# Column sums in layer 0, a scan in the recurrence: a change to a four-layer graph and feed-forward kernel

## The reference

```python
# layer 0, graph part (x is normalised first, the result is added to x)
h = layer_norm(x, ln_gamma, ln_beta)
agg = einsum('bij,bjh->bih', adj, h)
return x + relu(agg @ W_rel + b_rel + h @ W_root)

# layer 0, feed-forward part: a recurrence over T = 128 steps, batch 64
i_t = sigmoid(xi_t + h @ V_i)
g_t = tanh(xg_t + h @ V_c)
o_t = sigmoid(xo_t + h @ V_o)
c_new = h * c + i_t * g_t
h_new = o_t * tanh(c_new)

# layer 1, graph part: needs a sum over each row of adj
adj_norm = adj / (sum(adj, axis=-1, keepdims=True) + EPS)
```

## Time and profile before

| what | value |
|---|---|
| median of 3 runs | 1869.44 us (1867.50 to 1871.53) |
| span of the profiled execution | 1867.1 us |
| TensorE busy, share of the span | 1627.8 us, 87% |
| VectorE busy, share of the span | 1095.9 us, 59% |
| ScalarE busy, share of the span | 998.9 us, 53% |
| GpSimd busy, share of the span | 786.7 us, 42% |
| mean granted TensorE clock | 0.941 |

### The profile page before, as it was taken

One profiled execution on the slowest core, in us unless ns is written; L12 is line 12 of the kernel. 1 busy time (PEld: TensorE's weight loads), 2 busy tenths in 40 slices (PEclk: granted clock), 3 DMA queues, 4 the chain that ended last, 5 costly groups with the idle time before them and its releaser, 6 DMA issues. The chain is left out here.

```text
span 1867.1 us, 43356 instructions
## 1 busy us (share of the span) xinstructions
PE 1627.8 (87%) x13366; PEld 1314.2 (70%) x13366; DVE 1095.9 (59%) x4199; ACT 998.9 (53%) x3116; POOL 786.7 (42%) x1358
## 2 busy tenths in 40 slices
PE   7978899988859987999998888879999888884995
PEld 5756677767759985788887566679999845553542
DVE  7933433348737777699998755523333377763552
ACT  5854444446636656666665433246666534441663
POOL 6710000014426666111111677745565434554675
PEclk9989999999969999899999799989999989995998
DMA  3200000010014420000000511122222253105331
GB/s 114 84 1 1 1 1 1 1 27 1 1 36 134 123 80 1 2 3 2 2 3 3 156 47 48 62 62 70 72 71 72 56 150 86 58 24 88 100 86 35
DMA packets 125926, 91.76 MB, mean 49 GB/s; under 512 B 23591, under 2 KB 116554, under 8 KB 125701
## 3 DMA queue, kind: packets, MB, share of 16 engines
q1 hardware_dynamic: 109110, 61.89, 12.6%
q0 software_dynamic: 13568, 25.90, 4.3%
q10 hardware_dynamic: 3024, 1.21, 0.4%
HBM read 57.71 MB, written 33.30 MB: 49 GB/s over the span
## 5 line engine op out<-in xcount | busy, mean ns | idle before, releaser
L1361 ACT ACTIVATE FEAT<-BANKS,FEAT 128x128 f32<-128x128 f32 x544 | 155.5, 368 | 82.1 <-PE BANKS L1314 82.1
L1206 POOL DMA_INDIRECT scratch_made<-FEAT x136 | 144.9, 1065 | 122.6 <-DVE FEAT L1500 119.8
L1061 ACT ACTIVATE EXP<-BANKS,NEGMAX 128x128 f32<-128x128 f32 x512 | 139.4, 383 | 59.5 <-DVE NEGMAX L1073 59.5
L440 ACT ACTIVATE gates<-BANKS,EXP 128x64 f32<-128x64 f32 x384 | 97.4, 314 | 112.6 <-PE BANKS L417 112.6
L1314 PE MATMUL BANKS<-FEAT 128*128 128x128 f32 x1088 | 145.5, 277 | 0.0
L1323 PE MATMUL BANKS<-AUX,FEAT 128*128 x1088 | 144.5, 276 | 0.4 <-ACT FEAT L1361 0.4
L417 PEld LDWEIGHTS BANKS<-AUX,EXP 128*128 128x128 f32 x768 | 95.4, 191 | 69.7 <-DVE AUX L464 69.6
L1198 POOL DMA_INDIRECT scratch_sent<-FEAT,POS x128 | 125.1, 977 | 38.3 <-issue 37.5
L990 POOL COPY EXP<-AUX 128x32 f32<-128x32 f32 x256 | 42.5, 211 | 217.8 <-PE BANKS L1036 217.8
L1314 PEld LDWEIGHTS BANKS<-FEAT 128*128 128x128 f32 x1088 | 133.9, 194 | 0.0
L1323 PEld LDWEIGHTS BANKS<-AUX,FEAT 128*128 128x128 f32 x1088 | 133.2, 193 | 0.6 <-issue 0.6
(11 more groups left out here) (367 smaller groups left out, 4196.0 us busy)
## 6 DMA issues: line engine op xcount, KB each, us to landing
EXP<-in_L_ffn_W SPq DMA_DIRECT2D x128, 128.0 KB, 2.1
FEAT<-scratch_sent SPq DMA_DIRECT2D x136, 64.5 KB
EXP<-scratch_made SPq DMA_DIRECT2D x32, 256.0 KB, 3.4
FEAT<-scratch_sent SPq DMA_DIRECT2D x96, 65.5 KB, 1.9
X<-in_x SPq DMA_DIRECT2D x16, 256.0 KB, 2.9
STAGE<-in_adj SPq DMA_DIRECT2D x16, 256.0 KB, 3.3
scratch_sent<-NONE SPq DMA_DIRECT2D x48, 65.5 KB, 3.3
scratch_sent<-FEAT,POS POOLq DMA_INDIRECT x192, 2.3
```

The costliest lines, as they stand in the source:

```text
L440: act.activation(gates[:, at, sp_, :], PS[2 * at + par][:, u * B:(u + 1) * B], f, bias=wr["b" + gate]).then_inc(done, 1)
L1061: last = act.activation(tile(EXS[:, par], 4 * k + n), tile(PS[j], c), ACT.Exp, bias=NEGMAX[:, par, 4 * k + n:4 * k + n + 1])
L1206: pool.indirect_dma_start(out=made2, out_offset=bass.IndirectOffsetOnAxis(ap=XI_I[:, t % R_IN, H:ROW2], axis=0), in_=YO[:, t % R_OUT, :], ...
L1361: last = act.activation(tile(HR[:, t % R_H], c), tile(PS[2 + t % 2], c), ACT.Gelu, bias=BT[:, c, t:t + 1])
```

## The change

The column sums leave the recurrence: TensorE makes them in layer 0, four behind each group's adjacency products, into the same bank 6. In their place the recurrence issues a filler, so that every step has two fillers beside an input product or three without one. On VectorE, `ig` and `cell` become one `tensor_tensor_scan`, which runs along its 128 columns with state = `by` * state + `plus`. Column 2b of `by` is zero and of `plus` is g, so the state becomes g; column 2b + 1 of `by` is i and of `plus` is h times the old cell, so the state becomes the new cell. ScalarE therefore writes i and g, and VectorE `hc`, at every second column of a buffer, and the cell is read at every second column of `made`. GpSimd clears `made` and `by` at the start. The waits written ahead of the scan are `hc`, `it`, `gt`, in this order.

```diff
--- before.py
+++ after.py
@@ -217,6 +217,7 @@
                        "raw2 mv2 var2 rstd2 n2 m2 xn2 x_ps xT")
         adj_v = a["adj"].rearrange("(g b) i j -> g i b j", b=G)
         x_v = a["x"].rearrange("(g b) t h -> g t b h", b=G)
+        ROWSUM = PS[6][:, 0:B]
         PWB = sb("PWB", [P, 2, 2, 2, G])
         NMR = sb("NMR", [P, 2, G])
         NEG = sb("NEG", [P, 2, G])
@@ -368,6 +369,8 @@
                         last = pe.matmul(tile(PS[3], k), tile(WC2[:, par], k), cols(AT, i, GW, k * T, T),
                                          start=False, stop=True, skip_group_check=True)
                     last.then_inc(s.conv, 1)
+                    for k in range(G):
+                        pe.matmul(ROWSUM[:, G * i + k:G * i + k + 1], cols(AT, i, GW, k * T, T), ones[:, 0:1], start=True, stop=True)
 
                 def back(i, par, half):
                     pe.wait_ge(s.relu, i + 1)
@@ -382,20 +385,20 @@
                 unrolled(NG, [(2, hT), (3, back), (2, project), (0, adjacency), (4, xT), (2, conv)])
 
         layer()
-        s = sems("rnn", "zero x_even x_odd g i o gt it ot hc ig c ct h")
+        s = sems("rnn", "zero x_even x_odd g i o gt it ot hc c ct h")
         HS = AUX
-        cell = lb("cell", [P, 2, B])
-        hc = lb("hc", [P, 2, B])
-        ig = lb("ig", [P, 2, B])
-        gates = lb("gates", [P, 3, 2, B])
+        by = lb("by", [P, 2, B, 2])
+        plus = lb("plus", [P, 2, B, 2])
+        made = lb("made", [P, 2, B, 2])
+        gate_o = lb("gate_o", [P, 2, B])
         tanhc = lb("tanhc", [P, 2, B])
         NT = T // STEPS
-        ROWSUM = PS[6][:, 0:B]
         with nc.Block() as block:
             @block.gpsimd
             def _(pool):
                 pool.memset(HS[:, 0:B], 0.0).then_inc(s.zero, 1)
-                pool.memset(cell[:, 1, :], 0.0).then_inc(s.zero, 1)
+                pool.memset(made[:, 1], 0.0).then_inc(s.zero, 1)
+                pool.memset(by[:], 0.0).then_inc(s.zero, 1)
 
             @block.tensor
             def _(pe):
@@ -412,16 +415,14 @@
 
                     for u in range(STEPS):
                         step = j * STEPS + u
-                        pe.wait_ge(s.h if step else s.zero, step if step else 2)
+                        pe.wait_ge(s.h if step else s.zero, step if step else 3)
                         for gate_at, (gate, sem) in enumerate(zip("ico", (s.i, s.g, s.o))):
                             pe.matmul(PS[2 * gate_at + par][:, u * B:(u + 1) * B], wr["V" + gate],
                                       cols(HS, j, STEPS * B, u * B, B), start=False, stop=True,
                                       skip_group_check=True).then_inc(sem, 1)
                         if prefetch and u < 6:
                             inputs(j + 1, 1 - par, u // 2, u % 2)
-                        if step < B:
-                            pe.matmul(ROWSUM[:, step:step + 1], AT[:, step * T:(step + 1) * T], ones[:, 0:1], start=True, stop=True)
-                        for _ in range((2 if prefetch and u < 6 else 3) - (step < B)):
+                        for _ in range(2 if prefetch and u < 6 else 3):
                             pe.matmul(PS[7][:, 0:half], ident[:], cols(FEAT, j, STEPS * B, 0, half), start=True, stop=True)
                 for gate_at in range(3):
                     for part in range(2):
@@ -434,13 +435,15 @@
                 def turn(j, par):
                     for u in range(STEPS):
                         step, sp_ = j * STEPS + u, u % 2
-                        for at, (gate, made, done, f) in enumerate((("i", s.i, s.it, ACT.Sigmoid), ("c", s.g, s.gt, ACT.Tanh),
-                                                                    ("o", s.o, s.ot, ACT.Sigmoid))):
-                            act.wait_ge(made, step + 1)
-                            act.activation(gates[:, at, sp_, :], PS[2 * at + par][:, u * B:(u + 1) * B], f,
+                        for at, (gate, ready, done, f, into) in enumerate((
+                                ("i", s.i, s.it, ACT.Sigmoid, by[:, sp_, :, 1]), ("c", s.g, s.gt, ACT.Tanh, plus[:, sp_, :, 0]),
+                                ("o", s.o, s.ot, ACT.Sigmoid, gate_o[:, sp_, :]))):
+                            act.wait_ge(ready, step + 1)
+                            act.activation(into, PS[2 * at + par][:, u * B:(u + 1) * B], f,
                                            bias=wr["b" + gate]).then_inc(done, 1)
                         act.wait_ge(s.c, step + 1)
-                        act.activation(tanhc[:, sp_, :], cell[:, sp_, :], ACT.Tanh).then_inc(s.ct, 1)
+                        act.activation(tanhc[:, sp_, :], made[:, sp_, :, 1], ACT.Tanh).then_inc(s.ct, 1)
+                act.wait_ge(s.zero, 3)
                 for j in range(NT):
                     turn(j, j % 2)
 
@@ -451,19 +454,18 @@
                         step, q = j * STEPS + u, u % 2
                         if step:
                             v.wait_ge(s.h, step)
-                        v.tensor_tensor(hc[:, q, :], cols(HS, j, STEPS * B, u * B, B), cell[:, 1 - q, :],
+                        v.tensor_tensor(plus[:, q, :, 1], cols(HS, j, STEPS * B, u * B, B), made[:, 1 - q, :, 1],
                                         ALU.mult).then_inc(s.hc, 1)
+                        v.wait_ge(s.hc, step + 1)
+                        v.wait_ge(s.it, step + 1)
                         v.wait_ge(s.gt, step + 1)
-                        v.wait_ge(s.it, step + 1)
-                        v.tensor_tensor(ig[:, q, :], gates[:, 0, q, :], gates[:, 1, q, :], ALU.mult).then_inc(s.ig, 1)
-                        v.wait_ge(s.hc, step + 1)
-                        v.wait_ge(s.ig, step + 1)
-                        v.tensor_tensor(cell[:, q, :], hc[:, q, :], ig[:, q, :], ALU.add).then_inc(s.c, 1)
+                        v.tensor_tensor_scan(made[:, q].rearrange("p b k -> p (b k)"), by[:, q].rearrange("p b k -> p (b k)"),
+                                             plus[:, q].rearrange("p b k -> p (b k)"), 0.0, ALU.mult, ALU.add).then_inc(s.c, 1)
                         v.wait_ge(s.ot, step + 1)
                         v.wait_ge(s.ct, step + 1)
-                        v.tensor_tensor(cols(HS, j, STEPS * B, (u + 1) * B, B), gates[:, 2, q, :], tanhc[:, q, :],
+                        v.tensor_tensor(cols(HS, j, STEPS * B, (u + 1) * B, B), gate_o[:, q, :], tanhc[:, q, :],
                                         ALU.mult).then_inc(s.h, 1)
-                v.wait_ge(s.zero, 2)
+                v.wait_ge(s.zero, 3)
                 for j in range(NT):
                     turn(j, j % 2)
```

## The result

The changed kernel takes 1878.08 us (median of 4 runs, 1874.56 to 1880.98) where the kernel before takes 1870.01 us (median of 4): a ratio of 1.0043 with a 95% interval of 1.0026 to 1.006, so it is slower. The medians differ by 8.1 us, where the prediction forecast 3.7. The execution profiled has a span of 1872.7 us against 1867.1, 5.6 us more. Where these 5.6 us lie is read from the starts of two instructions, the relu of layer 0 and the last multiply of a step of the recurrence, in both kernels (for the last multiply before, see the earlier trace rows).

What follows compares the result with a forecast made beforehand. Layer 0 was taken as bound by a closed loop across several engines, the recurrence by a chain of dependent steps. Terms: 11.0 - 7.3 = +3.7 us, giving 1873.1 us; range 1862 to 1884.

Steps and rivals of the forecast that it cites:

- the worked-out case: Whole kernel: the summed terms give +3.7 us, 1873.1 us, own range 1870 to 1876; chance 0.58.
- (a): Recurrence, before the scan: the late wait costs nothing extra, -5 us in all, 1864; chance 0.08.
- (b): Layer 0: the column sums are absorbed, -7 us in all, 1862; chance 0.05.
- (d): Recurrence activations: ScalarE pays for strided access, +3 to +22 us on top, about 1883; chance 0.13.
- Column sums in layer 0, +11.0 us: Layer 0: sums delay hT and so L313 by 0.73 us; round 6.12 instead of 5.39, 15 x 0.73.
- Fillers, nothing: Recurrence, steps 0 to 63: one more filler each costs nothing unless a step falls below about 2.07 us.
- The scan, 0.425 us: VectorE in the recurrence: scan estimated at two slots a column, 0.425 us, between bounds 0.29 and 0.95.
- (c): Recurrence: the scan runs at the tensor_tensor row, 0.29 us; -13 us in all, 1856; chance 0.08.
- (e): Recurrence: the scan is longer than estimated, 1.3 us per 0.01 us, 1895 at 0.6 us; chance 0.08.
- The wait, 0.10 us: Recurrence, g's end to scan: late semaphore written last, so 0.10 us, not 0.03; saving 0.057 a step, -7.3 us.
- Strides, 0: Recurrence: writing or reading every second word taken as 0, bounds 0 and +22 us.
- lengthened activations: Recurrence, ScalarE: activations stay 0.314 and 0.256 us; the prediction is wrong if they lengthen.

Runs made afterwards that it cites:

- sums_behind_hT: Changed kernel with each group's column sums one round later, behind the next group's hT transposes; 1865.64 us against 1868.06 for the kernel before, ratio 0.999.
- gt_first: Changed kernel with the scan's waits written gt, hc, it; 1862.75 us against 1866.26 for the kernel before, ratio 0.9984.
- it_last: Kernel before, without a scan, with the waits of ig written it, gt instead of gt, it; 1876.72 us against 1866.26, ratio 1.0062.
- ct_first_before: Kernel before with the last multiply's waits written ct, ot instead of ot, ct; 1858.93 us against 1868.14, ratio 0.9943.
- two_waits: Changed kernel with the scan waiting for hc and gt only; 1872.06 us against 1866.24 for the kernel before, ratio 1.0038.
- sums_back: Changed kernel with the column sums in the recurrence again; two executions 1867.50 and 1868.47 us, four 1935 to 1939, beside 1866.26 for the kernel before.
- sums_back_table_early: Changed kernel, column sums back in the recurrence, ScalarE's cleared-buffers wait moved behind its first-gate wait; 1863.24 us against 1868.06 for the kernel before, ratio 0.9977.
- fewer_fillers: Changed kernel with one filler less in each of steps 0 to 63; 1878.52 us against 1868.06 for the kernel before, ratio 1.0054.

## Why the prediction was right, and where it was off

Direction and range hold: slower was the likeliest of the three, at 0.46, and 1878.1 lies within 1862 to 1884. The size does not. The forecast of +3.7 us is under half of the +8.1 measured, and 1878.1 lies outside the 1870 to 1876 to which the worked-out case gave 0.58; the wide range holds because it was drawn to take in rivals (a), (b) and most of (d), and none of them came. The mechanisms of both parts were right. What failed is the size of one term and one term that was missing.

- *Column sums in layer 0, +11.0 us*: measured +10.6, in the change and alone. The place (L313 waits for `hT`) and the round (6.12 forecast, 6.10 measured) hold. Rival (b) falls here; with the sums behind `hT` (sums_behind_hT) it comes true.
- *Fillers, nothing*: right in the step. The room was larger than worked out: at a step of 2.08 us TensorE's loads still wait 0.25 us for h.
- *The scan, 0.425 us*: measured 0.425. The half throughput that the Trainium skill states (DVE: opcode table, instruction layouts, handler registers and perf-mode slots, section 6, Datapath and trigger behaviour) agrees with it. Rivals (c) and (e) fall.
- *The wait, 0.10 us*: the term that was mis-sized. The mechanism is right (gt_first, it_last, ct_first_before) and rival (a) falls, but the gap is 0.13, since two semaphores are served ahead of the scan and not one (with one, in two_waits, it is 0.10). That is 0.03 x 128 = 3.8 us. The Trainium skill (Perfetto Trace Analysis, Identifying Dependency Chains) says that instructions which wait on several engines may have semaphore instructions inserted ahead of them; it gives no price, the runs do.
- *Strides, 0*: 5 ns on each of the two gates and 4 on tanh; of the gates' 5 ns the chain sees one, since the second starts at the same pitch. That makes about 0.009 us a step, 1.2 us. The prediction named lengthened activations as a sign that it is wrong; they lengthened, but by under a tenth of the 0.06 us that rival (d) has as its upper bound for one activation, and (d) falls.
- So a step saves 0.057 - 0.027 - 0.009 = 0.02 us: 2.7 us where 7.3 were counted.
- *ScalarE's wait for the cleared buffers*: the term that was missing. I costed the memset and not the new wait in front of the first activation, by which the table load came out in the open: 1.28 us for the load, 1.5 us between sums_back and sums_back_table_early.

Sum with the measured terms: 10.6 - 2.7 + 2.2 = +10.1 us, where 1.3 to 1.5 of the 2.2 are the table and the rest, about 0.7, the lower clock of that one execution. Without this rest the sum is some +9.4 us, beside +8.1 between the medians.

## What to carry to other kernels

When an instruction waits for several semaphores, write the one that comes last first: the instruction carries the first wait itself, and the others are served ahead of it. When the late one is among those served ahead, the start came 0.07 us later with one of them and 0.10 us later with two. On a chain of 128 dependent steps that was 9 to 12.5 us for the order of two or three lines. Work moved under another stage's cover is free only at a place where what is queued behind it has the slack: the same 64 sums cost 10.6 us in front of `hT` and nothing behind it. A wait written ahead of ScalarE's first activation can push the table load into the open, here 1.3 to 1.5 us.

## What the runs showed of the hardware

A scan over 128 columns took 0.425 us, 3.3 ns a column with its fixed part, where a two-input op on 128 columns takes 0.292. Writing at every second word cost ScalarE 5 ns on 64 columns (0.319 for 0.314 us). In one execution of fewer_fillers the granted clock fell back to its lower level soon after it had risen, behind a step in which TensorE had waited for the table. One kernel, sums_back, ran at a mean granted clock of 0.89 in four of six executions; why stays open.
